# Attention and a mixture of experts on one core: every engine's list of calls and every choice of bank set anew

## The reference

```python
def attn(x, Wq, Wk, Wv, Wo, gamma, beta):          # x is layernorm(input), 16 heads of 64
    q, k, v = (einsum('bsd,hde->bhse', x, W) for W in (Wq, Wk, Wv))
    scores = where(causal, einsum('bhse,bhte->bhst', q, k) / sqrt(64), -inf)
    out = einsum('bhst,bhte->bhse', softmax(scores), v)
    y = x + out.transpose(0, 2, 1, 3).reshape(B, S, 1024) @ Wo
    return layernorm(y, eps=1e-3) * gamma + beta

def ffn(x, gate_w, gate_up_w, down_w):             # x is layernorm of the sum, 32 experts, top 8
    probs = softmax(x @ gate_w.T)
    comb = top 8 of probs, divided by their sum, 0 elsewhere
    for each expert e:
        g, u = split(x @ gate_up_w[e].T)
        acc += (u * silu(g)) @ down_w[e].T * comb[:, e]
    return acc

x = x + attn(layernorm(x), ...)
x = x + ffn(layernorm(x), ...)
```

## Time and profile before

| | |
|---|---|
| median of 3 runs | 1696.54 us (1695.65 to 1697.38) |
| the profiled execution's own time | 1698.83 us |
| its span | 1697.0 us |
| mean granted TensorE clock | 0.990 |
| PE busy | 1611.1 us, 95% |
| VectorE (DVE) busy | 1428.4 us, 84% |
| POOL (GpSimd) busy | 1413.8 us, 83% |
| ScalarE (ACT) busy | 1399.0 us, 82% |
| DMA queue of SP, share of 16 engines | 53.6% |

### The profile page before, as it was taken

The page is one execution under the profiler, slowest core; times in us unless marked ns, Lnnn a source line. Parts: engine busy times, 40 slices in busy tenths (PEclk is TensorE's granted clock), DMA queues, the critical chain, the costliest instruction groups (busy, mean ns, idle before and its releaser), DMA issues.

```text
span 1697.0 us, 56373 instructions
## 1 busy us (share of the span) xinstructions
PE 1611.1 (95%) x21209; PEld 1104.6 (65%) x21209; DVE 1428.4 (84%) x4461; ACT 1399.0 (82%) x2371; POOL 1413.8 (83%) x1183
## 2 busy tenths in 40 slices
PE   4899999999999999999999999999999999999968
PEld 1476666667666666676667666666666666666645
DVE  7889789798888988888898888989888898888745
ACT  3999888888988888798888988888888888988852
POOL 0687897979889797997979889797998979889884
PEclk8899999999999999999999999999999999999989
DMA  9754544746556384544646555374654646355423
GB/s 252 162 115 109 145 115 127 170 116 157 123 135 140 103 183 102 155 111 129 161 115 163 124 133 136 107 185 115 155 111 131 146 120 163 86 145 139 112 85 108
DMA packets 213902, 228.55 MB, mean 135 GB/s; under 512 B 20480, under 2 KB 178432, under 8 KB 213376
## 3 DMA queue, kind: packets, MB, share of 16 engines
q1 hardware_dynamic: 213632, 224.94, 53.6%
HBM read 84.89 MB, written 5.24 MB: 53 GB/s over the span
## 4 chain that ended last, share of the span: by engine, by line
PE 35%; POOL 30%; issue 10%; SPq 8%; DMA 8%; ACT 7%; DVE 3%; POOLq 0%; ACTq 0%; DVEq 0%
POOL p_lo L1484 10%; PE bank_r L393 8%; POOL expert_room L1499 8%; POOL halves L1508 8%; PE bank_s L393 8%; PE bank_x L393 5%; PE bank_u L393 4%; PE bank_v L393 4%; PE bank_g L393 4%; DMA expert_room<-comb_rows 3%; DMA score_ops<-rowmaxT 3%; SPq L317 2%; SPq L316 2%; SPq L315 2%; ACT p L850 2%
## 5 line engine op out<-in xcount | busy, mean ns | idle before, releaser
L1484 POOL TENSOR_TENSOR p_lo<-p,p_hi 128x1280 f16<-128x1280 f32 x256 | 671.3, 2623 | 111.8 <-ACT p_hi L783 110.9
L850 ACT ACTIVATE p<-bank_s,back 128x512 f32<-128x512 f32 (+1 forms) x768 | 457.7, 613 | 88.1 <-PE bank_s L393 51.4
L393 PE MATMUL bank_s<-score_ops 128*128 128x62 f16 (+10 forms) x4096 | 398.7, 233 | 19.8 <-DMA score_ops<-rowmaxT 15.7
L393 PEld LDWEIGHTS bank_s<-score_ops 128*128 128x128 f16 x4096 | 275.2, 97 | 176.6 <-ACT p L850 34.1
L783 ACT ACTIVATE p_hi<-p 128x1280 f16<-128x1280 f32 x256 | 324.2, 1266 | 3.4 <-PE bank_r L393 1.2
L1499 POOL TENSOR_TENSOR expert_room<-expert_room 128x512 f32<-128x512 f32 x240 | 304.8, 1275 | 18.0 <-DMA expert_room<-comb_rows 12.4
L1508 POOL TENSOR_TENSOR halves<-expert_room,halves 128x512 f16<-128x512 f32 x240 | 277.4, 1160 | 2.4 <-ACT halves L783 1.6
L1125 DVE CUSTOM_DVE_ANT_0 max_junk<-bank_r,mask 128x512 f16<-128x512 f32 (+3 forms) x401 | 183.3, 490 | 20.6 <-PE bank_g L393 17.9
L393 PE MATMUL bank_x<-w_hi,halves 128*128 128x128 f16 x1920 | 195.8, 219 | 3.4 <-POOL halves L1508 3.3
L783 ACT ACTIVATE halves<-expert_room 128x512 f16<-128x512 f32 x240 | 150.3, 627 | 29.7 <-POOL expert_room L1499 15.2
L393 PE MATMUL bank_x<-w_lo,halves 128*128 128x128 f16 x960 | 171.7, 219 | 0.0
(11 more groups left out here) (287 smaller groups left out, 5018.0 us busy)
## 6 DMA issues: line engine op xcount, KB each, us to landing
score_ops<-nat SPq DMA_DIRECT2D x256, 256.0 KB, 3.9
score_ops<-nat SPq DMA_DIRECT2D x512, 128.0 KB, 3.9
expert_room<-comb_rows SPq DMA_DIRECT2D x240, 256.0 KB, 3.5
xt<-in_x SPq DMA_DIRECT2D x16, 256.0 KB, 4.7
xb<-in_x SPq DMA_DIRECT2D x16, 256.0 KB, 4.0
out_y<-expert_room SPq DMA_DIRECT2D x16, 256.0 KB, 3.6
score_ops<-comb_rows SPq DMA_DIRECT2D x16, 256.0 KB, 5.1
expert_room<-in_gate_up SPq DMA_DIRECT2D x1, 2048.0 KB, 10.6
```

Of the source, the lines that this page charges most:

```text
L393: return pe.matmul(dst, lhsT, rhs, start=start, stop=stop, skip_group_check=shared)
L850: act.activation(p32[:, h % P_SLOTS, at:at + cols], bank[score_bank(h, u)][:, 0:cols], ACT.Exp, scale=back[:, SC_SCORE:SC_SCORE + 1]).then ...
L1484: pool.tensor_tensor(p_lo[:, slot, :], p32[:, slot, :], p_hi[:, slot, :], ALU.subtract).then_inc(p_lo_done, 1)
```

## The change

All lists of the five engines and all letters of banks are set anew. The order was chosen by a replay of the program in which transfers land one after another in turn. Every call of before stands in the lists of after as often as it did; no operation, no shape, no transfer and no buffer changed, and the loop has the same form. Many calls moved by a few places. What the prediction speaks of is cut out of the diff here. First SP's loop:

```diff
             for n in range(2, B - 2):
-                load_x(n + 2); place_max(n, 1); spread_weights(n - 2, 15); place_qk(n, 5); place_max(n, 2)
-                place_qk(n, 6); place_qk(n, 7); load_xb(n); store(n - 2); keep_weights(n - 1); spread_weights(n - 1, 0)
+                place_max(n, 1); spread_weights(n - 2, 15); load_x(n + 2); place_qk(n, 5); place_max(n, 2); load_xb(n)
+                place_qk(n, 6); store(n - 2); place_qk(n, 7); keep_weights(n - 1); spread_weights(n - 1, 0)
                 spread_weights(n - 1, 1); spread_weights(n - 1, 2); spread_weights(n - 1, 3); spread_weights(n - 1, 4)
-                place_max(n, 3); spread_weights(n - 1, 5); spread_weights(n - 1, 6); spread_weights(n - 1, 7)
-                place_qk(n + 1, 0); place_qk(n + 1, 1); spread_weights(n - 1, 8); place_qk(n + 1, 2)
+                place_max(n, 3); spread_weights(n - 1, 5); place_qk(n + 1, 0); spread_weights(n - 1, 6)
+                spread_weights(n - 1, 7); place_qk(n + 1, 1); place_qk(n + 1, 2); spread_weights(n - 1, 8)
                 place_max(n + 1, 0); spread_weights(n - 1, 9); spread_weights(n - 1, 10); spread_weights(n - 1, 11)
                 place_qk(n + 1, 3); spread_weights(n - 1, 12); spread_weights(n - 1, 13); spread_weights(n - 1, 14)
                 place_qk(n + 1, 4)
```

Of PE's loop, its start, the stretch around turn_weights and turn_maxima(n, 3), and from turn_maxima(n+1, 0) to its end:

```diff
-                scores(n, 2, 1); scores(n, 2, 2); gate_product(n - 2, 13, R1); max_scores(n, 2, 0, R0, G)
-                up_product(n - 2, 12, V); scores(n, 3, 0); values(n, 4, R0); times_v(n, 1, V)
-                gate_product(n - 2, 14, G); scores(n, 3, 1); scores(n, 3, 2); max_scores(n, 2, 1, U, R1)
-                up_product(n - 2, 13, V); scores(n, 4, 0); values(n, 5, U); scores(n, 4, 1); scores(n, 4, 2)
...
-                gate_product(n - 1, 1, G); up_product(n - 1, 0, U); turn_weights(n - 1); scores(n, 10, 1)
-                up_product(n - 1, 1, U); turn_heads(n, 3, V); gate_product(n - 1, 2, G); up_product(n - 1, 2, R1)
-                times_v(n, 8, U); scores(n, 10, 2); max_scores(n, 3, 3, R0, G); scores(n, 11, 0); times_wo(n, 1, V)
-                max_scores(n, 3, 4, R1, U); scores(n, 11, 1); gate_product(n - 1, 3, G); max_scores(n + 1, 0, 0, R0, R1)
-                scores(n, 11, 2); up_product(n - 1, 3, U); times_v(n, 9, V); project(n + 1, 2, R0); values(n + 1, 1, R1)
-                gate_product(n - 1, 4, G); turn_heads(n, 4, V); values(n + 1, 2, R0); turn_maxima(n, 3, R1)
...
-                times_v(n, 13, R0); down_product(n - 1, 5); turn_maxima(n + 1, 0, V); gate_product(n - 1, 9, U)
-                scores(n, 15, 2); max_scores(n + 1, 1, 1, V, G); project(n + 1, 6, R0); up_product(n - 1, 8, R1)
-                up_product(n - 1, 9, V); project(n + 1, 7, U); gate_product(n - 1, 10, R1); down_product(n - 1, 6)
-                turn_heads(n, 6, V); scores(n + 1, 0, 0); scores(n + 1, 0, 1); times_v(n, 14, R0); scores(n + 1, 0, 2)
...
-                project(n + 1, 8, U); project(n + 1, 9, R1); gate_product(n - 1, 11, R0); times_wo(n, 3, G)
-                scores(n + 1, 2, 0); times_v(n + 1, 0, V); gate_product(n - 1, 12, G); up_product(n - 1, 11, R0)
-                turn_maxima(n + 1, 1, U); down_product(n - 1, 9); down_product(n - 1, 10)
...
+                scores(n, 2, 1); gate_product(n - 2, 13, R1); scores(n, 2, 2); up_product(n - 2, 12, U); scores(n, 3, 0)
+                times_v(n, 1, V); max_scores(n, 2, 0, R0, G); max_scores(n, 2, 1, U, R1); scores(n, 3, 1)
+                scores(n, 3, 2); values(n, 4, R0); gate_product(n - 2, 14, G); values(n, 5, U); up_product(n - 2, 13, V)
+                values(n, 6, R1); scores(n, 4, 0); down_product(n - 2, 11); scores(n, 4, 1); up_product(n - 2, 14, V)
...
+                up_product(n - 1, 0, U); scores(n, 10, 0); scores(n, 10, 1); turn_weights(n - 1)
+                up_product(n - 1, 1, U); turn_heads(n, 3, V); gate_product(n - 1, 2, G); scores(n, 10, 2)
+                up_product(n - 1, 2, R1); times_v(n, 8, U); scores(n, 11, 0); max_scores(n, 3, 3, R0, G)
+                times_wo(n, 1, V); max_scores(n, 3, 4, R1, U); scores(n, 11, 1); gate_product(n - 1, 3, G)
+                max_scores(n + 1, 0, 0, R0, R1); scores(n, 11, 2); up_product(n - 1, 3, U); times_v(n, 9, V)
+                project(n + 1, 2, R0); values(n + 1, 1, R1); gate_product(n - 1, 4, G); turn_heads(n, 4, V)
+                values(n + 1, 2, R0); turn_maxima(n, 3, R1); down_product(n - 1, 0); gate_product(n - 1, 5, U)
...
+                gate_product(n - 1, 8, G); times_v(n, 13, R0); scores(n, 15, 0); turn_maxima(n + 1, 0, V)
+                gate_product(n - 1, 9, R1); scores(n, 15, 1); max_scores(n + 1, 1, 1, V, G); project(n + 1, 6, R0)
+                down_product(n - 1, 5); scores(n, 15, 2); up_product(n - 1, 8, R1); up_product(n - 1, 9, V)
+                turn_heads(n, 6, G); scores(n + 1, 0, 0); project(n + 1, 7, U); scores(n + 1, 0, 1)
...
+                down_product(n - 1, 8); times_v(n + 1, 0, U); project(n + 1, 9, R1); scores(n + 1, 2, 0)
+                down_product(n - 1, 9); up_product(n - 1, 11, R0); times_wo(n, 3, U); turn_maxima(n + 1, 1, V)
+                gate_product(n - 1, 12, G); down_product(n - 1, 10)
```

POOL's loop:

```diff
-                residual_inverse(n - 1); weigh_unit(n - 2, 11); weigh_unit(n - 2, 12); p_low(n, 2); unit_low(n - 2, 11)
-                weigh_unit(n - 2, 13); unit_low(n - 2, 12); p_low(n, 3); p_low(n, 4); unit_low(n - 2, 13)
-                weigh_unit(n - 2, 14); p_low(n, 5); weigh_unit(n - 2, 15); unit_low(n - 2, 14); unit_low(n - 2, 15)
-                split_maxima(n, 2); p_low(n, 6); p_low(n, 7); second_inverse(n - 1); keep_h(n + 1); p_low(n, 8)
-                input_inverse(n + 2); p_low(n, 9); weigh_unit(n - 1, 0); weigh_unit(n - 1, 1); weigh_unit(n - 1, 2)
-                split_maxima(n, 3); unit_low(n - 1, 0); unit_low(n - 1, 1); p_low(n, 10); weigh_unit(n - 1, 3)
-                p_low(n, 11); unit_low(n - 1, 2); weigh_unit(n - 1, 4); unit_low(n - 1, 3); weigh_unit(n - 1, 5)
-                p_low(n, 12); add_beta(n); unit_low(n - 1, 4); weigh_unit(n - 1, 6); p_low(n, 13); unit_low(n - 1, 5)
-                split_maxima(n + 1, 0); weigh_unit(n - 1, 7); unit_low(n - 1, 6); p_low(n, 14); weigh_unit(n - 1, 8)
-                unit_low(n - 1, 7); p_low(n, 15); unit_low(n - 1, 8); weigh_unit(n - 1, 9); p_low(n + 1, 0)
-                weigh_unit(n - 1, 10); split_maxima(n + 1, 1); unit_low(n - 1, 9); unit_low(n - 1, 10); p_low(n + 1, 1)
...
+                weigh_unit(n - 2, 11); residual_inverse(n - 1); weigh_unit(n - 2, 12); unit_low(n - 2, 11); p_low(n, 2)
+                weigh_unit(n - 2, 13); p_low(n, 3); weigh_unit(n - 2, 14); unit_low(n - 2, 12); p_low(n, 4)
+                unit_low(n - 2, 13); p_low(n, 5); weigh_unit(n - 2, 15); unit_low(n - 2, 14); unit_low(n - 2, 15)
+                split_maxima(n, 2); p_low(n, 6); p_low(n, 7); second_inverse(n - 1); p_low(n, 8); add_beta(n)
+                input_inverse(n + 2); p_low(n, 9); weigh_unit(n - 1, 0); weigh_unit(n - 1, 1); unit_low(n - 1, 0)
+                weigh_unit(n - 1, 2); split_maxima(n, 3); unit_low(n - 1, 1); weigh_unit(n - 1, 3); p_low(n, 10)
+                p_low(n, 11); unit_low(n - 1, 2); unit_low(n - 1, 3); weigh_unit(n - 1, 4); p_low(n, 12)
+                weigh_unit(n - 1, 5); unit_low(n - 1, 4); keep_h(n + 1); weigh_unit(n - 1, 6); p_low(n, 13)
+                weigh_unit(n - 1, 7); split_maxima(n + 1, 0); unit_low(n - 1, 5); unit_low(n - 1, 6); p_low(n, 14)
+                unit_low(n - 1, 7); weigh_unit(n - 1, 8); p_low(n, 15); weigh_unit(n - 1, 9); unit_low(n - 1, 8)
+                p_low(n + 1, 0); unit_low(n - 1, 9); weigh_unit(n - 1, 10); split_maxima(n + 1, 1); unit_low(n - 1, 10)
+                p_low(n + 1, 1)
```

Of ACT's loop the lines with copy_weights, and of DVE's the last ones, with qk_low(n+1, 9):

```diff
-                gate_tanh(n - 1, 1, G); exps(n, 9, 2); exps(n, 10, 0); copy_weights(n - 1); v_high(n + 1, 0, R0)
...
+                exps(n, 9, 2); gate_tanh(n - 1, 1, G); v_high(n + 1, 0, R0); copy_weights(n - 1); exps(n, 10, 0)
...
-                add_heads(n, 3, G); qk_low(n + 1, 9, R1); denominators(n + 1, 0, V); residual_stats(n)
-                times_up(n - 1, 11, R0); divide(n + 1, 0, V)
...
+                times_up(n - 1, 11, R0); qk_low(n + 1, 9, R1); add_heads(n, 3, U); residual_stats(n)
```

More of the change, by code:

```diff
@@ L354, in _ @@
[L354 to L358, removed]
@@ L376, in _ @@
[L376 to L379, removed]
-            spread_weights(14, 6); spread_weights(14, 7); spread_weights(14, 8); spread_weights(14, 9); load_xb(15)
@@ new lines, in _ @@
+            turn_heads(0, 2, R1); max_scores(0, 3, 4, G, U); scores(0, 8, 0); scores(0, 8, 1); times_v(0, 6, R0)
+            scores(0, 8, 2); project(1, 2, U); scores(0, 9, 0); scores(0, 9, 1); project(1, 3, R0)
+            max_scores(1, 0, 0, V, R1); times_v(0, 7, G); scores(0, 9, 2); values(1, 0, U); scores(0, 10, 0)
+            turn_maxima(0, 3, V); scores(0, 10, 1); values(1, 1, R1); max_scores(1, 0, 1, R0, G); turn_heads(0, 3, U)
```

(23 more changed lines are left out.)

1005 lines of the change are left out of this document (494 added, 511 removed).

## The result

The changed kernel takes 1674.76 us, the median of 4 runs (1672.79 to 1676.33), against 1696.9 for the kernel before (4 runs, 1695.65 to 1697.38). The ratio is 0.987, 95% interval 0.9853 to 0.9887: 22 us, 1.3%, faster. The prediction was 1684 with a range of 1672 to 1704. The profiled execution has a span of 1672.4 us at a mean granted clock of 0.991, against 1697.0 at 0.990.

The account below looks back on a forecast made before the run. PE was taken as the bound (busy 1611.1 of 1697.0 us), POOL in the attention part's last 51 us. −17.3 + 7.2 − 2.2 − 1 = −13.3 on 1698.8 gave 1685.5, 1683.2 on the median, stated as 1684; range 1672 to 1704.

Parts of the forecast that it names:

- rival C: All goes as the order intends: waits gone, no new one at turn_maxima(n,3); 1674 us, chance 0.15.
- Maxima of group 0: First score of the next pass: place_max 2.09 us earlier, −0.83 for less PE work between; the 0.80 wait goes.
- Group 1: At scores(n,4,0): load_x behind place_max wins 0.74; net +1.4 against waits of 0.68, 0.85 on average: nearly gone.
- The term for both: PE's waits for placed row maxima, groups 0 and 1: 1.5 left of 18.8 us, −17.3 us.
- The term +7.2: At turn_maxima(n,3): unit_low(n−1,0) ahead of split_maxima and a later start make a new wait, 12×0.6 = +7.2 us.
- turn_weights: PE's wait of 0.4 us there: scores(n,10,1) moves ahead of it, gaining PE up to 0.1 a pass.
- POOL's full stretch: POOL, without gap from 985.42 to 1026: add_beta leaves, keep_h comes in, −0.66 us; times_v(n,13) costs 0.
- the cover: The 0.66 us from add_beta leaving POOL's full stretch, covering times_v(n,13)'s wait; without it 0.7 a pass.
- The shorter way of 1.60: PE's way from that head's last score to times_v(n,13), from 9.27 to 7.67 us; alone, a wait of 0.68.
- rival D: Slower: POOL's full stretch becomes the bound and passes on a late start; 1710 us, range 1702 to 1712, chance 0.20.
- Runs of max_scores: PE's loop: 120 in place of 144 places where max_scores follows another kind of call, 24×0.09 = −2.2 us.
- Prologue and epilogue: Before and after the loop: prologue −1 us within bounds ±2; epilogue 0, ±2.

Follow-up runs that it names:

- b_lx2q: The kernel before with place_qk(n+1,0) ahead of spreads 6 and 7 and load_x(n+2) directly behind place_max(n,1) in SP's loop: 1681.26 us, ratio 0.9922.
- a_split: The kernel after with unit_low(n-1,0) moved behind split_maxima(n,3) in POOL's loop, as before: 1675.98 us, ratio 0.9886.
- a_pool: The kernel after with POOL's loop of before: 1718.51 us, ratio 1.0136.
- b_head: The kernel before with all five prologues of after, and the bank of turn_maxima(2,1) as the loop of before wants it: 1691.98 us, ratio 0.9982.

## Why the prediction came out as it did

The direction, the mechanism and the range were right; the size was low, 13 of 22 us. What came is nearly the number of the rival C, which I had put at 1674 with 0.15. Its reason isn't what came: it had the weights land and weigh_unit start earlier, and weigh_unit(n−1, 0) starts where it did (below).

**Maxima of group 0.** Right in every part: place_max(10, 0) follows its copy by 0.07, the wait is gone, and the one call place_qk(n+1, 0) does it. The −0.83 for PE's shorter way was right as well: put back, the wait costs 1.60, where 0.66+0.83 = 1.49 would be expected.

**Group 1.** The wait is gone. The reason given was half right. Moving place_max ahead of load_x works (b_lx2q), but I had costed it without its reader: input_stats had 1.1 us to spare at best and nothing in some passes, and moved as far as the change moves it, in the lists of before, it costs 37 us. The change moved input_stats too, and I had not looked at that.

**The term for both**, −17.3: the count gives 12×1.49 = −17.9, and moving two calls in before (b_lx2q) 14 by the timed runs.

**turn_maxima(n, 3), the step that failed.** The term +7.2 was mis-sized: 12×0.08 = 1 was measured, and a_split, which takes away its cause, is no faster than after (1675.98 and 1674.76). I had passed a later copy_weights on in full to POOL's start: copy_weights ends 0.11 later from turn_h2 on average in after (7.83, not 7.72), but weigh_unit(n−1, 0) starts at 13.99 after turn_h2 as it did at 14.04. The slack was also taken from one pass: in the pass of the earlier trace rows split_maxima ends 19.14 after turn_h2, on average 18.64, so PE had 1.4 to spare and not 1.00. The move of unit_low takes 1.07 of it. I had read the latest pass of ten.

**turn_weights.** Forecast a gain of up to 0.1 a pass. The wait of 0.61 went whole, and 0.48 came at up_product(n−1, 0), which waits for gate_times_tanh on DVE; another 0.31 at max_scores(n, 3, 2), which wants a bank that turn_h's readers hold. I had no row for either. Together −0.61+0.48+0.31−0.09 (turn_h2) = +0.09, a loss of 1 us in 12 passes and not a gain: next to nothing either way, but neither the sign nor the reason was right. The wait at turn_weights in before and that at up_product in after both stand behind turn_h2's readers on ACT and DVE; that the order only chooses at which call PE waits for them is my reading, and no run tests it.

**POOL's full stretch.** No wait at times_v(n, 13), as forecast, but the cover wasn't needed. With POOL's loop of before, where add_beta is back in that stretch (a_pool), p_low(n, 13) ends 0.68 later after turn_h2 (40.67, not 39.99), as priced, and times_v(n, 13) starts at 40.90 and still has 0.23 to spare; I had it waiting 0.68. The shorter way of 1.60 was the part that was too large: times_v(n, 13) starts 0.92 earlier in after (40.94, not 41.86). POOL's order mattered more than I had priced, at readers that I hadn't looked at: down_product, times_v(n, 3) and the scores of heads 3 and 4. The rival D, a late start passed on through the whole stretch, was wrong for this kernel, and the exchanges of POOL's loop don't show it either: their waits come at calls that stand late in one list for where their readers stand in another, most of them outside the stretch.

**Runs of max_scores.** −2.2 forecast, 12×0.23 = −2.8 measured. The count of places was wrong: the loops have 15 and 14 such places a pass, not 12 and 10. One place less at 0.09 explains 1 us of it; the rest of these 2.8 us I can't name, so that the size came out was luck.

**Prologue and epilogue.** −1 forecast, −4 measured by b_head; the epilogue 0, as forecast.

The sum was 13.3 us of gain. With 6 too much of a loss at turn_maxima and 3 too little of a gain for the prologue, the two errors make the difference to the measured 22. It was right to take off the 2.3 us by which the profiled execution of before lay above its median: the medians of before were 1695.4 to 1696.9 on all chips.

## What to carry to other kernels

A transfer that is late can be late at its issue: compare the end of what it waits for with its place in the queue's timeline, and look for a call ahead of it that stands waiting for something else; moving six issues into such a hole was worth 8 us in one order and 19 in another. When a load is moved back in a queue, find its reader on the other engine and its slack first, because with a slack of 1 us or less 7 us of hoped gain turned into 37 of loss. And take slack from all passes, not from the one pass whose rows are at hand: at turn_maxima(n, 3) the pass that I read had 1.0 us where the mean was 1.4, and at input_stats it had 1.0 where the mean was 0.5.
